# A spiking RWKV block with a split-precision feed-forward on one core: orders laid over five groups, remainders of the activations all on VectorE

## The reference

```
x = x + layernorm(attn(layernorm(x)))
x = x + layernorm(ffn(layernorm(x)))

attn(x):   x = x + lif(time_mix(ln1(x)));  x = x + lif(channel_mix(ln2(x)))
time_mix:  xx = x shifted by one step;  xk, xv, xr = blends of x and xx
           k = xk @ Wk; v = xv @ Wv; r = sigmoid(xr @ Wr)
           return (r * wkv(w_decay, u, k, v)) @ Wo     # weighted sum over time, with a running maximum
channel_mix: k = relu(xk @ fWk)**2;  return sigmoid(xr @ fWr) * (k @ fWv)
lif:       v = v/2 + x/2;  s = (v >= 1);  v = v * (1 - s)   # step by step in time
ffn(x):    h = silu((x @ w1.T) * s1) * ((x @ w2.T) * s2)    # 128 -> 512
           h = gelu((h @ h1.T) * sh1); h = gelu((h @ h2.T) * sh2)  # 512 -> 512, exact gelu
           return (h @ w3.T) * s3                            # 512 -> 128
```

## Time and profile before

| what | us |
|---|---|
| median of three runs (lowest, highest) | 771.79 (770.97, 773.90) |
| the profiled execution, its own time | 772.1 |
| its span, first to last instruction | 770.3 |
| PE busy, 2563 matmuls | 633.8 |
| DVE busy, 1558 instructions | 605.6 |
| ACT busy, 711 | 478.7 |
| POOL busy, 560 | 433.5 |

### The profile page before, as it was taken

How to read it: one execution, slowest core, us unless ns; L and a number is a source line. 1 busy time by engine, 2 the same in 40 slices (tenths; PEclk the granted TensorE clock), 3 DMA queues, 4 the chain that set the end, 5 groups by cost and what they waited for, 6 DMA issues and landing times. The chain is left out here.

```text
span 770.3 us, 10620 instructions
## 1 busy us (share of the span) xinstructions
PE 633.8 (82%) x2563; PEld 398.7 (52%) x2563; DVE 605.6 (79%) x1558; ACT 478.7 (62%) x711; POOL 433.5 (56%) x560
## 2 busy tenths in 40 slices
PE   3175399889898989889898989899898979888894
PEld 1022146565564646455564646565565646465663
DVE  5888777988879697897979797988979797955340
ACT  2543376767666674767667675857677676847461
POOL 4333526666574765666674767566665757553432
PEclk9567689999999999999999999999999999999998
DMA  6020000000000000000000000000000000000000
GB/s 205 4 69 0 29 1 2 27 16 28 14 29 15 12 16 14 27 14 27 14 27 14 27 9 5 27 14 27 14 27 14 14 15 14 15 1 1 14 15 14
DMA packets 26528, 16.70 MB, mean 22 GB/s; under 512 B 1152, under 2 KB 25728, under 8 KB 26240
## 3 DMA queue, kind: packets, MB, share of 16 engines
q1 hardware_dynamic: 26496, 16.34, 7.0%
HBM read 12.14 MB, written 4.19 MB: 21 GB/s over the span
## 5 line engine op out<-in xcount | busy, mean ns | idle before, releaser
L718 ACT ACTIVATE hid<-p_f,scale 128x512 f32<-128x512 f32 x128 | 87.9, 687 | 119.5 <-PE p_f L1490 119.5
L412 POOL TENSOR_TENSOR var<-mv,eps_row 128x4 f32<-128x4 f32 x64 | 34.4, 537 | 188.4 <-DVE mv L945 188.4
L1490 PE MATMUL p_f<-a_lo,w_hi 128*128 128x512 f32 x256 | 112.1, 438 | 9.3 <-DVE a_lo L295 8.6
L1490 PE MATMUL p_f<-b_lo,w_hi 128*128 128x512 f32 x256 | 109.1, 426 | 2.8 <-DVE b_lo L295 1.2
L1490 PE MATMUL p_f<-a_hi,w_hi 128*128 128x512 f32 x256 | 104.6, 409 | 0.0
L1490 PE MATMUL p_f<-b_hi,w_hi 128*128 128x512 f32 x256 | 101.1, 395 | 0.0
L425 POOL TENSOR_TENSOR rstd<-var,minus_half 128x4 f32<-128x4 f32 x64 | 81.9, 1279 | 2.5
L1475 PE MATMUL p_m<-kk,mix 128*128 128x512 f32 x128 | 64.9, 613 | 9.4 <-ACT kk L692 9.2
L1466 PE MATMUL p_m<-mixed,mix 128*128 128x512 f32 x128 | 65.1, 633 | 6.5 <-issue 6.1
L1490 PEld LDWEIGHTS p_f<-a_lo,w_hi 128*128 128x128 f32 x256 | 50.5, 197 | 30.7 <-DVE a_lo L295 13.5
L1537 PEld LDWEIGHTS p_turn<-w,hid 128*128 128x128 f32 x512 | 58.7, 192 | 10.7 <-issue 9.3
(11 more groups left out here) (132 smaller groups left out, 1541.9 us busy)
## 6 DMA issues: line engine op xcount, KB each, us to landing
xa<-in_x SPq DMA_DIRECT2D x16, 256.0 KB, 2.9
xb<-in_x SPq DMA_DIRECT2D x16, 256.0 KB, 3.2
out<-y_out SPq DMA_DIRECT2D x16, 256.0 KB, 2.3
kk<-in_ffn SPq DMA_DIRECT2D x1, 1024.0 KB, 6.6
hid<-in_ffn SPq DMA_DIRECT2D x1, 1024.0 KB, 9.0
mix<-in_mix SPq DMA_DIRECT2D x1, 512.0 KB, 6.6
hid<-in_ffn SPq DMA_DIRECT2D x1, 512.0 KB, 3.8
mix<-in_mix SPq DMA_DIRECT2D x1, 320.0 KB, 4.2
```

Of the source, the lines that this page charges most:

```text
L718: act.activation(hid[:, m], p_f[m % 2][:, :], ACT.Gelu, scale=scale[:, 1 + layer, m:m + 1]).then_inc(s_gelu[layer], 1)
L1490: last = pe.matmul(out_, w[:, b], x[:, k], start=(k == 0 and t == 0), stop=(k == n - 1 and t == len(terms) - 1))
```

## The change

It does five things.

1. The lists of all engines are written anew over five groups a turn. `schedule` runs i = -2 to 19, with 6 to 13 as the loop; `on` and the groups are now indexed by lag: `g[k]` is group i-k, for k from -2 to 4. A turn begins and ends elsewhere in a group's life: `stats_1` and `moments_1` of group i+1 and `norm_1` of group i are in one turn of DVE, and the first three `hidden(1)` are in the turn before the fourth.
2. `POOL_BLOCKS` is empty: DVE makes all four `low` blocks of both layers.
3. The weights' third part is staged in `gate` instead of `hid`, so its load waits for nothing; each part has semaphores of its own, and the counting is done by ACT as a sum of absolute values (`rest_weights`). All three parts are through in turn 1.
4. `gate_products` becomes `to_gate` and `to_value`, and the waits on PE for a free bank are written for the new order, with `after`. In turns outside the loop there are more of these than in the loop.
5. `s_bv` becomes two semaphores, and `moments_1` waits for `s_neg_mean[1]` in place of `s_x1`.

The core of the diff, and then the order that it makes at three places:

```diff
-POOL_BLOCKS = {1: (1,), 2: (1,)}
+POOL_BLOCKS = {1: (), 2: ()}
...
+def after(eng, sem, n, per=1, nth=1):
+    if isinstance(n, int):
+        if n < 0:
+            return
+        if n >= GROUPS_IN_ALL:
+            n, nth = GROUPS_IN_ALL - 1, per
+    eng.wait_ge(sem, per * n + nth)
...
-        parts = [(kk, H1, HB * HB), (hid, H2, HB * HB), (hid, W1, 2 * HB)]
+        parts = [(kk, H1, HB * HB), (hid, H2, HB * HB), (gate, W1, 2 * HB)]
...
-        def schedule(fori, first_turn, turn, last_turn, first=-1, last=GROUPS + 2):
+        def schedule(fori, first_turn, turn, last_turn, first=-2, last=GROUPS + 3):
...
-            loop = range(4, GROUPS - 2)
+            loop = range(6, GROUPS - 2)
...
+            def rest_weights(k):
+                staged, blocks = part(k)
+                act.wait_ge(s_lo_w[k], 1)
+                act.activation(staged, w_lo[:, blocks].bitcast(F32), ACT.Abs,
+                               accum_out=w_rest[:, k:k + 1]).then_inc(s_rest[k], 1)
...
             def moments_1(g):
                 wait(dve, s_n[1], g.n)
-                wait(dve, s_x1, g.n)
+                wait(dve, s_neg_mean[1], g.n)
                 moments(1, g, bn1, mv1)
...
-            def count_weights(i):
-
-                staged, blocks = part(i + 1)
-                dve.wait_ge(s_lo_w, i + 2)
-                dve.tensor_scalar(staged, w_lo[:, blocks].bitcast(F32), 0.0, None, ALU.not_equal, ALU.add,
-                                  accum_out=w_rest[:, i + 1:i + 2]).then_inc(s_rest, 1)
...
                 def turn_1(g):
                     pe.wait_ge(s_n[1], g.n + 1)
-                    wait(pe, s_f0_lo, g.n - 2)
-                    wait(pe, s_f_out, g.n - 3)
+                    after(pe, s_f_out, g.n - 4)
+                    if isinstance(g.n, int):
+                        after(pe, s_f0_lo, g.n - 3)
+                        after(pe, s_z2, g.n - 2)
+                        after(pe, s_z1, g.n - 1)
                     turned(1, g, n1)
...
+                def rest_sum():
+                    pe.wait_ge(s_rest1, 1)
+                    pe.matmul(p_f[0][:, 0:1], ones16[:, :], w_rest1[:, :], start=True,
+                              stop=True).then_inc(s_rest_sum, 1)
...
-            program(False, last=1)
-            pe.wait_ge(s_rest1, 1)
-            pe.matmul(p_f[0][:, 0:1], ones16[:, :], w_rest1[:, :], start=True, stop=True).then_inc(s_rest_sum, 1)
+            program(False, last=2)
```

More of the change, by code:

```diff
@@ new lines, in turn @@
+            def turn(g, on):
+                if on[0]:
+                    norm_0(g[0])
+                if on[1]:
+                    weighted_sum(g[1], 0)
+                if on[4]:
+                    variance(5, g[4])
+                    rstd(5, g[4])
+                if on[0]:
+                    shift_1(g[0])
+                if on[-1]:
+                    variance(1, g[-1])
+                    rstd(1, g[-1])
+                if on[2]:
+                    neurons(1, g[2])
+                if on[4]:
+                    norm_5(g[4])
+                    residual_5(g[4])
+                if on[1]:
+                    neurons(0, g[1])
+                if on[2]:
+                    variance(3, g[2])
+                    rstd(3, g[2])
+                if on[1]:
+                    variance(2, g[1])
+                    rstd(2, g[1])
+                if on[2]:
+                    norm_3(g[2])
+                    residual_3(g[2])
+                if on[1]:
+                    shift_2(g[1])
+                if on[2]:
+                    variance(4, g[2])
+                    rstd(4, g[2])
+                if on[0]:
+                    weighted_sum(g[0], 1)
@@ new lines, in last_turn @@
+            def last_turn(g, on):
+                if on[1]:
+                    weighted_sum(g[1], 0)
+                if on[4]:
+                    variance(5, g[4])
+                    rstd(5, g[4])
+                if on[2]:
+                    neurons(1, g[2])
+                if on[4]:
+                    norm_5(g[4])
+                    residual_5(g[4])
+                if on[1]:
+                    neurons(0, g[1])
+                if on[2]:
+                    variance(3, g[2])
+                    rstd(3, g[2])
+                if on[1]:
+                    variance(2, g[1])
+                    rstd(2, g[1])
+                if on[2]:
+                    norm_3(g[2])
+                    residual_3(g[2])
+                if on[1]:
+                    shift_2(g[1])
+                if on[2]:
+                    variance(4, g[2])
+                    rstd(4, g[2])
@@ new lines, in scaled_w3, with low_weights @@
+            def scaled_w3():
+                dve.wait_ge(s_w3_in, 16)
+                dve.wait_ge(s_w3_row, 1)
+                for m in range(HB):
+                    last = dve.tensor_tensor(w3[:, m], w3[:, m], p_f[1][:, 0:P], ALU.mult)
+                last.then_inc(s_w3_scaled, 1)
+            def low_weights(k):
+                staged, blocks = part(k)
+                dve.wait_ge(s_hi_w[k], 1)
+                dve.tensor_tensor(w_lo[:, blocks], staged, w_hi[:, blocks].bitcast(F32),
+                                  ALU.subtract).then_inc(s_lo_w[k], 1)
@@ L935, in statistics, with rest_max @@
+            def rest_max():
+                for k in range(len(parts)):
+                    dve.wait_ge(s_rest[k], 1)
+                dve.tensor_reduce(w_rest1[:, :], w_rest[:, :], AX_X, ALU.max).then_inc(s_rest1, 1)
             def statistics(n, g, bn, tiles):
```

1580 lines of the change are left out of this document (884 added, 696 removed).

## The result

The changed kernel takes **728.02 us** (median of 4 runs, 726.62 to 728.71) beside 772.75 us for the kernel before on the same chip (4 runs): a ratio of 0.9421, 95% interval 0.9395 to 0.9447. The profiled execution took 728.21 us, 726.1 of them span, so the two traces differ by 770.3 - 726.1 = 44.2 us.

What follows compares the result with a forecast made beforehand. The order of handing work between TensorE and VectorE bounds the kernel, not an engine. Start -7.0, middle -33.8, clock -1.5 and tail -2.5 make -44.8 from 772.1: 727 us, range 708 to 752 (about 0.8).

Steps and rivals of the forecast that it cites:

- Steady turn: One turn of the loop: 42.6 us falls to 40.0, a gain of 2.6, over 13 intervals -33.8 us.
- PE without its waits needs 42.6 - 4.4 = 38.2: Loop turn: taking TensorE's 4.4 us of waits off the turn leaves 38.2 us as its floor.
- VectorE busy: Loop turn: VectorE's busy time goes from 37.0 to 37.5 us, with +1.35 for remainders and -0.85 for the normalisation.
- The term for `n1`: VectorE in a loop turn: this normalisation, moved ahead of `f0_lo`, gets faster beside GpSimd's small vectors: -0.8 us.
- Start: Up to the first gate product: seven terms sum to -7.0 us, bounds -12 and +2.
- the other five terms: Start, besides counts: `out_product` earlier -2.7, `rest_sum` +1.7, `k_product` before `fired_sum(0)` +1, `rstd2` earlier -1, branch -1.3 us.
- `rest_sum`: Start, TensorE before `turn_1` of group 1: it waits for ScalarE's counts of all three parts, +1.7 us.
- The same work: Tail: work unchanged, only remainders faster on VectorE than GpSimd, two groups by two layers by 0.6: -2.5 us.
- Little gained: Rival: removed waits return as new ones in the cycle around one group; turn 41.7, 751 us; chance 0.15.
- no difference: Rival: the loop is only cut elsewhere, start gains eaten by two more turns of filling and draining; 772 us; chance 0.04.
- VectorE as the bound: Rival: VectorE's waits stay and two remainders add 1.3 us to each of 16 groups; 786 us; chance 0.06.
- The floor rival: Rival: the waits vanish and TensorE and VectorE both run at 38.4 us a turn; 706 us; chance 0.15.

Runs made afterwards that it cites:

- experiment 3: Changed kernel with each split activation's second remainder back on GpSimd: 738.57 us; kernel before with all four remainders on VectorE: 768.38 us.

## Why the prediction held, and where it didn't

Forecast 727, measured 728. That the two are 1 us apart is luck: inside the middle two errors of opposite sign nearly cancelled, the tail and the clock were off as well, and the move of the remainders, which the sum had as a load on VectorE, brings a third of the gain. What held is the mechanism, that the order of handing over bounds the turn and not an engine, and that the new order takes away most of TensorE's waits.

- **Steady turn (40.0, measured 38.70).** TensorE's remaining waits were put at 1.8 to 2.0 and are 1.8, but not by the sum as written: its terms add up to 2.8, and the overlap of 0.8 to 1.0 taken off them has no row behind it. The step that failed is "PE without its waits needs 42.6 - 4.4 = 38.2": the busy time is 36.91, not what it was (37.93). In the earlier trace rows TensorE stops eight times, in the changed kernel four times. My reading is that a stop costs beyond its idle time, since the products behind it overlap less: by (37.93 - 36.91) / 4 to 5 some 0.2 to 0.25 us each, an estimate from these rows. The other runs' turns mostly fit it (three stops and 36.82 us busy with GpSimd's product moved, five and 37.36 with remainders on GpSimd, six and 37.39 with `n1` back); the old order with all remainders on VectorE doesn't (eight stops, 38.34), so it isn't shown. The floor I gave (38.2 to 38.4) was no floor, and the plain turns gained 13 x 1.3 = 17 us more than the sum had.
- **VectorE busy (37.5, measured 36.05).** The term that was mis-sized is the remainders': the two cost +0.5, not +1.35, since the others became faster when GpSimd stopped (`a_lo` 3.0 us for three, 2.6 for four; `b_lo` 2.0 and 2.9). The term for `n1` was right (-0.9 for -0.85). The remaining half us is spread over many groups of instructions and traced to none. The 37.01 of before is sound: cut at the gate products instead, its steady intervals show 36.98 to 36.99.
- **Waits one by one.** `numerator` 0.6: right. `xres` 0.4, measured 0.7; `rstd4` 0.3, measured 0.6; `n4` before its transposes 0.3, measured 0.6; `spikes_turned(1)` 0.9, measured 0.5, with 0.5 for the `mixed` before it, which I had inside; `b_lo` 0.3, measured 0.2; `a_lo` 0.9: none at all, since the three come at 0.62 each; spikes of neuron 0 0.3: none.
- **The loop's jump.** Not in the sum: +8.7 us. Nothing in the profile of before shows it, but what the change does to the place of the loop could have been counted. Together with the 4.7 us of the first and the last interval, which the sum took for plain ones, it used up most of those 17.
- **Clock.** Of three dips in the middle I let one go; there are two: the intervals from 339.18 and from 577.2 show 0.96, the first of them behind a stall of the loop.
- **Start (-7.0, measured -5.9).** The counts were -4.7 (-2.3, -2.4) and are -5.5; what is left of the other five terms is -0.4, and they summed to -2.3. `rest_sum` (+1.7) costs nothing that the run with it later could show, and the branch gives 2.0 of its 6.1. For `out_product` the trace of before does say how much earlier `yr` was ready (done at 65.05, the product at 67.85, with `fired_sum(1)` at 67.75 in between, so the -2.7 was there to be had); what of it arrived, and how the remaining terms split, wasn't tried.
- **Tail (-2.5, measured +0.3).** The step that failed is "The same work", by which only the remainders counted. Their term was even too small: in the new order they are worth nearly 5 us of the tail (112.3 against 107.5, experiment 3), not 2.5. But with the remainders still on GpSimd the new order's tail is 112.3 where the old one's was 107.2, at a mean clock of 0.93 and 0.95. That the rest of the new order costs up to 5 us there is a term that the sum put at nothing; its extra turn of draining is the likely cause and was not tested. (In the old order the same move of the remainders left the tail at 110.4.) The run with VectorE written out has 105.8, with one dip of the clock less.
- **Rivals.** Little gained and no difference are out by the time. VectorE as the bound is out by experiment 3, in the old order too. The floor rival (turn 38.4) came nearest in the plain turn, but not for its reason: 1.8 us of waits are left, and the work under them is shorter than I had it. The Trainium skill's rule (Perfetto Trace Analysis, section Identifying the Most-Contended Engine), by which VectorE was to be relieved first, was no guide here: in the new order two subtractions fewer left VectorE busier (37.01 against 36.05 us a turn) and the kernel 18 us slower. Its sentence that work moved between VectorE and GpSimd might not help (section Optimizing Scalar/DVE Operations) agrees with the old order (0.998) and with that run, in which moving work to GpSimd did harm; the move the other way gained 18 us.

## What to carry to other kernels

Subtracting an engine's waits from a turn doesn't give its floor: here TensorE's busy time fell by 1.0 us together with its waits, by my reading because each stop also takes some of the overlap of the work around it. When a change lengthens what stands before a hardware loop or in it, look in the trace for instruction packets inside the loop and for idle time with "issue" at its first instruction; writing that engine's loop out, or shifting its begin by some empty instructions, is worth a try before anything is tuned. And moving work to the busier engine can be right when the other one is slower at it and slows both, as in the new order here; measure it in the order it is meant for, since in the old one it brought nothing.

## What the hardware showed unexpectedly

- A jump back on VectorE costs nothing or 2.0 to 3.0 us by where the loop's body begins; 40 empty instructions gave 7.5 us back, 8 took 9.8. The place of a loop is a thing that any edit before it can change.
- A remainder of 128x512 on GpSimd (1.29 to 1.68 us) makes the VectorE instructions beside it slower: the three `a_lo` take 1.0 us each on average instead of 0.67, one `mixed` 1.70 instead of 0.74. In the new order giving two of them to VectorE lowered its busy time by 1.0 us a turn (37.01 to 36.05).
- VectorE's straight code is fetched without a stall: with its loop written out it got 5 packets of 8 KB in 160 us (300 to 460), none of which lengthened a turn. TensorE behind its branch is another case: it stands 4.17 us in the changed kernel.

The fastest versions are the two at 717.96 us, 10 us under the changed kernel and 7% under the one before.
